# Attention pipeline of a two-layer transformer kernel: copies and high parts at other exponentials, totals ahead of the first output product of a block, output tiles and norm chunks two steps on

## The reference

```python
h = norm(x, cond)                       # layer norm, scale and shift from the condition
scores = q @ k.T / sqrt(32)             # per head, 1024 x 1024
a = softmax(scores, axis=-1)
x = x + (a @ v) @ wo                    # second layer: times a gate
h = norm2(x, cond)
x = x + gelu(h @ w1 + b1) @ w2 + b2     # second layer: times a gate
```

## Time and profile before

| | us |
|---|---|
| Median of three runs | 3954.56 (3951.26 to 3955.85) |
| The profiled execution | 3957.61 |
| Its span, first to last instruction | 3955.8 |
| PE busy | 3746.3 (95%) |
| VectorE busy | 2471.2 (62%) |
| ScalarE busy | 1603.8 (41%) |
| POOL busy | 1613.5 (41%) |

### The profile page before, as it was taken

One profiled execution on the slowest core, in us unless ns is written; L12 is line 12 of the kernel. 1 busy time (PEld: TensorE's weight loads), 2 busy tenths in 40 slices (PEclk: granted clock), 3 DMA queues, 4 the chain that ended last, 5 costly groups with the idle time before them and its releaser, 6 DMA issues.

```text
span 3955.8 us, 76367 instructions
## 1 busy us (share of the span) xinstructions
PE 3746.3 (95%) x31828; PEld 1559.4 (39%) x31828; DVE 2471.2 (62%) x3951; ACT 1603.8 (41%) x2807; POOL 1613.5 (41%) x907
## 2 busy tenths in 40 slices
PE   7988999999998989999899999999999999999999
PEld 4422444333543335433354333433344333543344
DVE  5677735766457755467654777467664776467752
ACT  1466313554125642155521663136621563126621
POOL 2467212672216742066510672137520672126611
PEclk8899999999999999999999999999999999999999
DMA  5233243212423123431232112311123112311122
GB/s 153 48 99 119 85 107 81 72 55 84 109 76 87 41 91 91 106 75 53 100 101 83 34 42 89 115 44 29 65 96 98 31 40 81 114 54 26 63 67 96
DMA packets 139110, 306.67 MB, mean 78 GB/s; under 512 B 19680, under 2 KB 59636, under 8 KB 137872
## 3 DMA queue, kind: packets, MB, share of 16 engines
q10 hardware_dynamic: 50944, 174.62, 13.6%
q1 hardware_dynamic: 87824, 127.17, 12.1%
HBM read 223.46 MB, written 36.66 MB: 66 GB/s over the span
## 4 chain that ended last, share of the span: by engine, by line
PE 79%; DVE 7%; POOL 5%; issue 4%; ACT 3%; DMA 1%; ACTq 0%; SPq 0%; POOLq 0%; DVEq 0%
PE ps L931 15%; PE ps L834 12%; PE ps L835 12%; PE ps L836 12%; PE ps L1029 9%; PE ps L871 7%; PE ps L1044 5%; PE ps L888 3%; POOL sums L730 3%; ACT probs L1209 3%; DVE mcol L1532 2%; PE ps L947 2%; PE ps L852 1%; DVE ring L1582 1%; DVE turn L1466 1%
## 5 line engine op out<-in xcount | busy, mean ns | idle before, releaser
L1532 DVE TENSOR_REDUCE mcol<-ps 128x1 f32<-128x512 f32 x2048 | 1290.0, 683 | 441.2 <-PE ps L931 226.7
L730 POOL TENSOR_TENSOR sums<-probs 128x1024 f32<-128x1024 f32 x448 | 1065.2, 2392 | 943.0 <-PE ps L1044 510.9
L1209 ACT ACTIVATE probs<-ps 128x512 f32<-128x512 f32 x2048 | 1098.8, 608 | 812.0 <-PE ps L931 564.3
L931 PE MATMUL ps<-qs,ks 98*32 98x512 f16 x8192 | 800.6, 389 | 105.4 <-ACT probs L1209 93.5
L931 PE MATMUL ps<-ks,qs 97*32 97x512 f16 x7040 | 697.3, 385 | 53.7 <-DVE mcol L1532 41.5
L1355 ACT ACTIVATE sums<-ps,cols 128x512 f32<-128x512 f32 x256 | 175.8, 687 | 1097.0 <-PE ps L836 1097.0
L1029 PE MATMUL ps<-probs,v_sb 128*32 128x512 f32 x4096 | 548.5, 612 | 0.0
L931 PEld LDWEIGHTS ps<-qs,ks 98*32 98x32 f16 x8192 | 215.5, 97 | 589.9 <-ACT probs L1209 363.9
L834 PE MATMUL ps<-ring,probs 128*128 128x512 f16 x1024 | 388.0, 379 | 0.3 <-DVE probs L1627 0.3
L834 PE MATMUL ps<-aT,ring 128*128 128x512 f16 x1024 | 388.1, 379 | 0.0
L836 PE MATMUL ps<-aT,ring 128*128 128x512 f16 x1024 | 388.0, 379 | 0.0
(11 more groups left out here) (112 smaller groups left out, 3471.9 us busy)
## 6 DMA issues: line engine op xcount, KB each, us to landing
ring<-halves ACTq DMA_DIRECT2D x208, 512.0 KB, 3.3
qs<-hl SPq DMA_DIRECT2D x192, 128.0 KB, 4.1
ring<-halves SPq DMA_DIRECT2D x48, 512.0 KB, 6.2
ring<-in_weights ACTq DMA_DIRECT2D x39, 512.0 KB, 4.6
halves<-ring ACTq DMA_DIRECT2D x37, 512.0 KB, 2.9
ks<-hl SPq DMA_DIRECT2D x120, 128.0 KB, 4.4
dcopy<-inverses SPq DMA_DIRECT2D x56, 256.0 KB
probs<-in_x SPq DMA_DIRECT2D x8, 1024.0 KB, 8.3
```

Source lines behind the costliest of these rows:

```text
L730: pool.tensor_tensor(sums[:, m % SUM_SLOTS, :, :], prob(u - 2), prob(u), ALU.add).then_inc(sum_set[0].sem, 1)
L931: mm = pe.matmul(bank[cut, :], lhs[:, cut], rhs, start=True, stop=True)
L1209: act.activation(prob(u)[:, e, :], ps[:, w % SCORE_BANKS, :], ACT.Exp).then_inc(exp_done.sem, 1)
L1532: dve.tensor_reduce(mcol[:, blk % 2, 4 * j + qt, half:half + 1], src, AX.X, ALU.max).then_inc(n_free[0], 1)
```

## The change

`O_AT` goes from 7 to 11, so the output product of a block is copied four exponentials later, after the last exponential of a block's third step. `HI_AT` goes from 11 to 19 and `LO_AT` from 1 to 4: the high part and the low part of the block before are made later. `WO_AT` goes from 53 to 55 and `LN2_AT` from 60 to 62: all four output tiles and all four norm chunks are two steps on, on every engine. In the step in which the first product of a block is due (the third of the block, in blocks 1 to 7), PE does the totals of that step first and the product after them. The transpose of the maxima is written as a matmul by the identity matrix, in fp32.

```diff
-O_AT, D_AT, HI_AT, INVERT_AT, NORM_AT, LO_AT = 7, 12, 11, 4, 6, 1
+O_AT, D_AT, HI_AT, INVERT_AT, NORM_AT, LO_AT = 11, 12, 19, 4, 6, 4
...
-WO_AT = 53
-LN2_AT = 60
+WO_AT = 55
+LN2_AT = 62
...
-                pe.transpose(bank[0:16, 0:P], mfin[:, :], ident[:, :]).then_inc(n_full, 1)
+                pe.matmul(bank[0:16, 0:P], mfin[:, :], ident[:, :], start=True, stop=True).then_inc(n_full, 1)
...
-                    if LAG <= u < UNITS + LAG:
+                    first = u > LAG and (u - LAG) % 16 == 0
+                    if LAG <= u < UNITS + LAG and not first:
                         values(i, u - LAG)
                     for pair in range(SUMS // 2):
                         if s == totals_step(i, pair):
                             totals(i, 2 * pair)
+                    if first:
+                        values(i, u - LAG)
                     some(rows_at(i, s))
```

## The result

Timed beside each other in six runs each, the changed kernel takes 3965.85 us (3962.68 to 3973.9) and the kernel before 3955.41 (3951.26 to 3957.92): ratio 1.0027, 95% interval 1.0016 to 1.0038, so 0.27% or 10.4 us slower. The profiled execution took 3966.32, its span is 3964.5.

A forecast was written before the change was run, and what follows sets the result against it. PE was taken to bound the kernel, busy 95% of the span. Block starts +2.0, plain matmul +6.8, tail waits -26.4 and clock +21.6 sum to +4.0: median 3958.6 us from 3954.6, forecast range 3948 to 3969, wider range 3934 to 3980.

The forecast's parts named there:

- that chain: End of attention, score 250 through norm chunks, sums and totals to first feed-forward matmul: 14.0 us, PE work 8.6, 5.4 lost.
- Block starts: First steps of attention blocks: later copy and totals first net 0.0 at 40 of 48 starts, +2.0 us in all.
- return from totals first: Block starts: totals end earlier, so POOL's next sum starts earlier and scores two steps on regain about 0.3 per start.
- Cost nothing: Moving the high and low parts fits in ScalarE's and POOL's slack and costs nothing, with +-5 us kept for reshuffling.
- loss to the later copy: Block starts: PE's product waits 0.82 for the copy behind exponential 11, so 0.33 us is lost per start.
- Plain matmul: 64 transposes of the maxima as plain fp32 matmuls: a second pass of 0.107 each, +6.8 us.
- the sign of being right: At each plain matmul, two rows, and the next tile 0.31 us after the first of them instead of 0.21.
- Waits of the tail: Steps 54 to feed-forward: moved output tiles and norm chunks gain 4.9 per first-layer pass, 1.7 per second-layer pass, -26.4 us.
- Clock: Half clock after new waits: 13.6 us in feed-forward matmuls of eight passes, 8 after step 60 in half the passes, +21.6.
- rival "slower": Wait ahead of feed-forward: slow stretch twice as long costs 14 more, step-60 wait in all passes 8 more: 3980; chance 0.15.
- The 3.0 per pass: Second layer, steps 59 and 63: half-clock time of the kernel before, 1.5 stretches of about 2.0 per pass, that would go.
- Tail with its clock: End of attention: the waits' -26.4 and the clock's +21.6 together; by layer -8.8 and +4.0.

The follow-up runs named there:

- part 1: Kernel before with `O_AT` 11, `HI_AT` 19, `LO_AT` 4 and totals ahead of a block's first product; alone 1.0024, +9.5 us.
- part 3: Kernel before with output tiles at steps 55 to 58 (`WO_AT` 55) and norm chunks at 62 and 63 (`LN2_AT` 62); alone 1.005, +19.8 us.
- sum 57 first: Kernel after the change, with VectorE's sum of exponentials 57 made ahead of its residual and norm work in step 58; 1.002 of the kernel before, +7.9 us.
- kernel with `LN2_AT` 61: Kernel after the change with VectorE's sum 57 ahead of its norm work and norm chunks at steps 61 and 62; 0.993 of the kernel before, -27.7 us.

## Why the prediction was right or wrong

The time came inside the range, 7 us above the forecast; the direction was forecast as "no change" and is slower by 0.27%. The pass ends as foretold: the first feed-forward matmul starts 14.7 after score 250 (3324.41 - 3309.67), where 14.0 was forecast. (The terms of that chain add up to 13.8, and PE's work in it to 8.2 and not 8.6; the 5.4 lost becomes 5.6.) Term by term:

- **Block starts, +2.0.** Measured +9.5. The return from totals first was right (-14.4 forecast, -14.2 measured). The step that failed is "Cost nothing" for `HI_AT` and `LO_AT`, measured +5.1 (interval 0.5 to 2.2 thousandths, 2 to 9 us), at the edge of the 5 us kept for it. The loss to the later copy was forecast at 0.33 x 48 = 16 (wait 0.82 less 0.53, and rounding) and is 9.5 + 14.2 - 5.1 = 18.6: the wait is 0.97, since the copy takes 0.65 at that place, not 0.60, and the product follows its end by 0.15, not 0.06.
- **Plain matmul, +6.8.** Measured -0.8. Two passes of 0.11 are in the trace (3669.80 and 3669.91), so the count was right; "in PE's order, with nothing beside it" was wrong: the next tile starts with the plain matmul, not 0.31 after it as the sign of being right had it. The price came from rows of full-width and totals work, and the neighbours of this tile are quarter-width.
- **Waits of the tail, -26.4.** The new waits were forecast well: 2.6, 0.27, 0.27 in step 60 (2.5, 0.27, 0.27 measured) and 3.7 ahead of the last totals (3.2 + 0.17). In the first layer the wait in step 60 is 1.8, less than forecast. The -26.4 isn't all waiting, though: 23.6 of it are half-clock stretches of the kernel before that were to go (4 x 2.9 and 4 x 3.0). The waits alone were to give 8.0 in the first layer and cost 5.2 in the second. From exponential 208 (step 52) to the first GELU, PE's idle time over four passes fell by 5.3 in the first layer and grew by 4.1 in the second, with 0.7 per pass of the time after for the wait for the copy, which is part 1's.
- **Clock, +21.6.** The last totals' wait did bring half clock in all eight passes. In the second layer it lasted from 3321 to 3327.5, across the totals and seven feed-forward matmuls, about twice the 3.4 forecast: that half of the rival "slower" came true there. Against it, the wait in step 60 brought half clock in two passes, not four. What the clock gives back was mis-sized too. The 3.0 per pass were read from pass 6 of the kernel before, which has about 7 us at half clock from exponential 208 on; passes 4 and 5 have about 3.5. In that stretch the second layer's time at half clock went from about 20 to 34 us, the first layer's from about 27 to 17.
- **Tail with its clock, -4.8.** Within the change it is 10.7 - 9.5 + 0.8 = +2.0, a difference of three measured ratios and good to 7 us. From exponential 208 to the first GELU, the profiled execution after is 8.2 us faster in the four first-layer passes and 8.3 slower in the four of the second layer, 0 in all. The forecast by layer was -8.8 and +4.0 (a gain of 4.9 or 1.7 per pass, less 2.7 of clock). So the first layer's gain came. The second layer's error is in the clock: PE's busy time there rose by 4.2, where the clock was to take 1.2 off. (Exponential 208 is taken since 212 waits for POOL's sum in the first-layer passes of the kernel before, 2.77 in pass 0, and a stretch that begins there leaves out an output tile of PE's work; other starts move these sums by 2 or 3 us.) By itself part 3 costs 19.8, as the forecast of its waits held only with `HI_AT` 19 and the copy's wait in front of it. That coupling, 14 us or more, isn't in the prediction at all: the cover named for the high and low parts was POOL's and ScalarE's slack, and VectorE's slowing beside POOL was missed though it stood in the trace of before (an application of 1.39 beside L768 in each first-layer pass).

So three errors of 7 or 8 us, two up and one down, left the sum 7 off; the closeness of 3958.6 is partly luck. The tail's error by the ratios is what the other two leave of the whole, so the sum is no check of it; by the profile it is about 5. Small terms in the sum didn't mean small parts: part 3 alone is +20, totals first alone -14, the later copy alone +83.

## What to carry to other kernels

Where two parts of a change meet, price each with the other absent as well as present: the later copy costs 83 us or 19 depending on whether the totals come first, and the tail 20 or 2 depending on where a 1.2 us operation of POOL falls. When a wait is removed from the middle of a chain that ends a stage, look for what ends the chain: moving VectorE's sum ahead mostly moved the wait, and putting the chain's head one step earlier gave 35 us. A copy that holds up other work can go later as long as its reader still finds it done; of the three places run here with the totals first, two exponentials after the old one did best, and four, by the estimate above, cost more than it gave. When an operation is moved, look again at what it now runs beside: POOL and VectorE met again in two of the later kernels, once at another place.

## What the runs showed of the hardware

- **VectorE beside POOL.** A one-input fp32 operation of VectorE (L1433, 128x512) takes 0.55 by itself and 1.38 when POOL's L768 (1.16) begins 0.06 ahead of it. In the first-layer passes of the kernel with `HI_AT` 11 VectorE's began 0.06 *ahead* of POOL's by the trace, and it took 1.50, while POOL's still took 1.16. The Trainium skill, "SBUF — State Buffer", section "Who interferes with whom", says of VectorE in its two-port modes (which `tensor_scalar` between tiles in SBUF can enter) that whichever of the two issues first gets the shared pair of ports for the whole instruction and the other blocks fully. The 1.38 agrees only in part: VectorE ended at 3315.54, 0.28 after POOL, where an operation begun only then would need its 0.55. The 1.50 doesn't show the first one winning, though starts on POOL are rough in the profile. With two inputs each, either can lose (kernel with sum 57 first, pass 6). POOL's L768, begun 0.07 behind VectorE's sum (3298.41, 1.22 as usual), took 2.16 and ended 1.01 after it. VectorE's L1457, begun 0.08 behind POOL's L762, took 1.74 and ended 0.56 after it.
- **A narrow matmul runs beside its neighbours.** The 16-column fp32 matmul started at the same 3669.80 as three quarter-width matmuls of the next tile; the transpose of the same shape left 0.10 before it and took 0.21.
- **Not every wait costs clock.** 3.23 with nothing in it, ahead of the last totals, was followed by 0.50 in 39 of the 40 passes of five kernels; the other (sum 57 first, pass 2) kept 1.00. 1.62 ahead of the totals in step 63, in the kernel with `LN2_AT` 61, was not (1.00 throughout). The wait in step 60 (2.3 in the second layer, 1.6 in the first) was followed by 0.50 in passes 6 and 3, and not in the other six; with `HI_AT` 11 back (3.16 and 2.55) it was in all eight.
